# A decoder layer on one core: activations quantised in three passes, through 16-bit integers in the result's place

## The reference, cut to what matters

```python
def _sym_qdq(x, scale):
    s = jnp.clip(jnp.abs(scale), 1e-09, None)
    return jnp.clip(jnp.round(x / s), -(Q_MAX + 1), Q_MAX) * s      # Q_MAX = 7
# _chunk_decompose, on chunks of 64 rows, per chunk and channel
ch_bias = (jnp.max(xp, axis=1, keepdims=True) + jnp.min(xp, axis=1, keepdims=True)) / 2
xz = xp - ch_bias
tmax = jnp.max(jnp.abs(xz), axis=(1, 2)); cmax = jnp.max(jnp.abs(xz), axis=1)
scale = tmax[:, None] / 2.0 ** (DECOMP - 1 - idx) / Q_MAX           # idx from cmax against tmax
result = _sym_qdq(xz, scale[:, None, :])
```

## Time and profile before

| | |
|---|---|
| median of 3 runs | 997.08 us (995.59 to 998.17) |
| the profiled execution | 992.63 us |
| its span, first to last instruction | 990.9 us |
| TensorE, VectorE, ScalarE, GpSimd busy | 757.2, 769.6, 628.0, 116.2 us |
| mean granted clock of TensorE | 0.869 of full speed |

### The profile page before, as it was taken

The page is one execution under the profiler, slowest core; times in us unless marked ns, Lnnn a source line. Parts: engine busy times, 40 slices in busy tenths (PEclk is TensorE's granted clock), DMA queues, the critical chain, the costliest instruction groups (busy, mean ns, idle before and its releaser), DMA issues.

```text
span 990.9 us, 15387 instructions
## 1 busy us (share of the span) xinstructions
PE 757.2 (76%) x5149; PEld 318.5 (32%) x5165; DVE 769.6 (78%) x1055; ACT 628.0 (63%) x1066; POOL 116.2 (12%) x218
## 2 busy tenths in 40 slices
PE   1576988999999999999934824544565559999997
PEld 0432322222222222222311214334334424444443
DVE  7999777999999999999599988688978883632111
ACT  4879435989888888899519217656666746752000
POOL 1200842000000000011000010000002140000001
PEclk9877997999999999999966856567768759999999
DMA  8500864122121212111030001100004830000000
GB/s 297 212 1 1 262 200 129 48 55 56 50 59 49 60 47 58 49 53 33 18 130 0 1 0 43 43 21 22 1 12 176 334 85 1 1 1 2 30 22 32
DMA packets 45733, 66.70 MB, mean 67 GB/s; under 512 B 8940, under 2 KB 23276, under 8 KB 45176
## 3 DMA queue, kind: packets, MB, share of 16 engines
q1 hardware_dynamic: 44408, 61.92, 19.5%
q0 software_dynamic: 1280, 4.20, 1.3%
HBM read 42.50 MB, written 19.14 MB: 62 GB/s over the span
## 4 chain that ended last, share of the span: by engine, by line
PE 50%; DVE 20%; ACT 18%; issue 6%; DMA 3%; POOL 1%; SPq 0%; ACTq 0%; POOLq 0%; DVEq 0%
PE PS L1450 12%; PE PS L1654 8%; PE PS L1665 8%; PE PS L1335 6%; PE PS L1467 6%; ACT slab L1770 4%; ACT slab L1706 2%; PE PS L1364 2%; PE PS L1582 2%; ACT HB L1757 2%; DMA slab<-in_L_ffn_w 2%; DMA slab<-in_x 1%; DVE mx L1039 1%; DVE mx L1038 1%; ACT slab L1677 1%
## 5 line engine op out<-in xcount | busy, mean ns | idle before, releaser
L905 DVE TENSOR_REDUCE SWV<-PS 128x2 f32<-128x1024 f32 x256 | 302.0, 1219 | 16.8 <-PE PS L1335 14.5
L1770 ACT ACTIVATE slab<-PS 128x512 f32<-128x512 f32 x512 | 275.7, 595 | 40.5 <-PE PS L1467 31.5
L1450 PE MATMUL PS<-slab,HB 128*32 128x256 f32 x2048 | 164.3, 393 | 9.9 <-ACT HB L1757 9.6
L1467 PE MATMUL PS<-slab 50*128 50x512 f16 x512 | 125.5, 385 | 3.7 <-ACT slab L1770 1.2
L1335 PE MATMUL PS<-slab 48*128 48x512 f16 x512 | 101.8, 392 | 6.3 <-DVE SWV L905 4.9
L1654 PE MATMUL PS<-slab 128*128 128x512 f16 x384 | 86.2, 388 | 1.7 <-DVE slab L1224 1.4
L1665 PE MATMUL PS<-slab 128*128 128x512 f16 x384 | 83.0, 379 | 0.0
L1450 PEld LDWEIGHTS PS<-slab,HB 128*32 128x32 f32 x2048 | 41.6, 108 | 91.1 <-issue 64.9
L1256 DVE SCALAR_TENSOR_TENSOR WOT<-PS,cmax,WOT 128x512 f32<-128x512 f32 x8 | 6.0, 751 | 69.8 <-PE PS L1665 69.8
L1335 PEld LDWEIGHTS PS<-slab 48*128 48x128 f16 x512 | 24.7, 93 | 104.8 <-issue 95.4
L605 POOL COPY HB<-slab 128x64 f32 (+1 forms) x128 | 24.5, 236 | 285.0 <-PE PS L1450 284.9
(11 more groups left out here) (305 smaller groups left out, 1196.8 us busy)
## 6 DMA issues: line engine op xcount, KB each, us to landing
slab<-in_L_ffn_w SPq DMA_DIRECT2D x2, 4096.0 KB, 14.7
q_split<-slab SPq DMA_DIRECT2D x24, 256.0 KB, 2.7
k_split<-slab SPq DMA_DIRECT2D x24, 256.0 KB, 2.7
slab<-q_split SPq DMA_DIRECT2D x64, 96.0 KB, 2.5
slab<-k_split SPq DMA_DIRECT2D x64, 96.0 KB, 2.5
slab<-in_x SPq DMA_DIRECT2D x4, 1024.0 KB, 12.3
slab<-HB SPq DMA_DIRECT2D x128, 32.0 KB
slab<-in_fside_BxS2xS SPq DMA_DIRECT2D x4, 1024.0 KB, 5.5
```

Source lines behind the costliest of these rows:

```text
L905: nc.vector.tensor_reduce(NM[:, ring].rearrange("p (a x) -> p a x", a=2)[:, :, x], PS[:, bank:bank + 2, :], AX.X, ALU.max, negate=True).th ...
L1450: ins = nc.tensor.matmul(PS[32 * h:32 * h + 32, 6, cols], VST[:, r % 2, k, h, :], PROB[:, k, h, cols], start=k == half == 0, stop=k == KB ...
L1467: nc.tensor.matmul(PS[:, st_bank(2 * s + a), :], KP[rows, r, p, P * k:P * k + P], QP[rows, r, p, :], start=True, stop=True).then_inc(st_re ...
L1770: nc.scalar.activation(PROB[:, k, 2 * a + p], PS[:, st_bank(t), :], ACT.Exp, scale=score_scale).then_inc(probs, 1)
```

## The change

The passes become three on both engines. "scale" and "round" become one: the difference is multiplied by the scale inverse and written as 16-bit integers into the bytes where the bf16 result will stand, the conversion doing the rounding. "back" reads the integers there and writes bf16 over them. On ScalarE the second set of activations has the function Copy with a scale per partition and no bias operand, writes integers, and the single activation at L1710 goes. Since `PASSES` has three entries, VectorE's loops change with it: in the first quantisation `scaled(3)` no longer stands ahead of the last pass but comes after `quantise` and the cast at L900.

```diff
-        PASSES = ("bias", "scale", "round", "back")
+        PASSES = ("bias", "round", "back")
...
-                    if kind == "scale":
-                        own(nc.vector.tensor_tensor(v, v, bc(s["inv"][:, lo:hi]), ALU.mult))
+                    whole = QTF[:, CHUNK * lo:CHUNK * hi]
                     if kind == "round":
-                        own(nc.vector.tensor_scalar(part, part, ROUND, ROUND, ALU.add, ALU.subtract))
+                        own(nc.vector.tensor_tensor(by_chunk(whole.bitcast(I16)), v, bc(s["inv"][:, lo:hi]), ALU.mult))
                     if kind == "back":
-                        nc.vector.tensor_tensor(by_chunk(QTF[:, CHUNK * lo:CHUNK * hi]), v, bc(s["pws"][:, lo:hi]),
+                        nc.vector.tensor_tensor(by_chunk(whole), by_chunk(whole.bitcast(I16)), bc(s["pws"][:, lo:hi]),
                                                 ALU.mult).then_inc(q_dve, 1)
...
-                for bias, scale in ((small["ind"], None), (None, small["inv"])):
-                    if scale:
-                        act.wait_ge(qs_ready, k)
-                    for q in range(lo, hi):
-                        part, _ = quantised(q, q + 1)
-                        nc.scalar.activation(part, part, ACT.Identity, bias=bias[:, q:q + 1] if bias else rnd[:, 0:1],
-                                             scale=scale[:, q:q + 1] if scale else 1.0).then_inc(q_step, 1)
-                    count_q[0] += hi - lo
-                    act.wait_ge(q_step, count_q[0])
-                nc.scalar.activation(a, a, ACT.Identity, bias=rnd[:, 1:2]).then_inc(q_step, 1)
-                count_q[0] += 1
+                for q in range(lo, hi):
+                    part, _ = quantised(q, q + 1)
+                    nc.scalar.activation(part, part, ACT.Identity, bias=small["ind"][:, q:q + 1]).then_inc(q_step, 1)
+                count_q[0] += hi - lo
+                act.wait_ge(q_step, count_q[0])
+                act.wait_ge(qs_ready, k)
+                for q in range(lo, hi):
+                    part, _ = quantised(q, q + 1)
+                    nc.scalar.activation(QTF[:, CHUNK * q:CHUNK * q + CHUNK].bitcast(I16), part, ACT.Copy,
+                                         scale=small["inv"][:, q:q + 1]).then_inc(q_step, 1)
+                count_q[0] += hi - lo
                 act.wait_ge(q_step, count_q[0])
                 for q in range(lo, hi):
-                    part, _ = quantised(q, q + 1)
-                    ins = nc.scalar.activation(QTF[:, CHUNK * q:CHUNK * q + CHUNK], part, ACT.Copy,
-                                               scale=small["pws"][:, q:q + 1])
+                    part = QTF[:, CHUNK * q:CHUNK * q + CHUNK]
+                    ins = nc.scalar.activation(part, part.bitcast(I16), ACT.Copy, scale=small["pws"][:, q:q + 1])
                 ins.then_inc(q_act, 1)
```

More of the change, by code:

```diff
@@ L20 @@
 NI = B * NG
+I16 = mybir.dt.int16
 KB = S // P
@@ L1698, in quantise @@
                 lo, hi = Q_DVE, Q_DVE + Q_ACT
-                a, _ = quantised(lo, hi)
                 act.wait_ge(qb_ready, k)
-                for bias, scale in ((small["ind"], None), (None, small["inv"])):
-                    if scale:
-                        act.wait_ge(qs_ready, k)
-                    for q in range(lo, hi):
-                        part, _ = quantised(q, q + 1)
-                        nc.scalar.activation(part, part, ACT.Identity, bias=bias[:, q:q + 1] if bias else rnd[:, 0:1],
-                                             scale=scale[:, q:q + 1] if scale else 1.0).then_inc(q_step, 1)
-                    count_q[0] += hi - lo
-                    act.wait_ge(q_step, count_q[0])
-                nc.scalar.activation(a, a, ACT.Identity, bias=rnd[:, 1:2]).then_inc(q_step, 1)
-                count_q[0] += 1
+                for q in range(lo, hi):
[9 more added lines that the diff above has]
+                count_q[0] += hi - lo
                 act.wait_ge(q_step, count_q[0])
                 for q in range(lo, hi):
-                    part, _ = quantised(q, q + 1)
-                    ins = nc.scalar.activation(QTF[:, CHUNK * q:CHUNK * q + CHUNK], part, ACT.Copy,
-                                               scale=small["pws"][:, q:q + 1])
+                    part = QTF[:, CHUNK * q:CHUNK * q + CHUNK]
+                    ins = nc.scalar.activation(part, part.bitcast(I16), ACT.Copy, scale=small["pws"][:, q:q + 1])
                 ins.then_inc(q_act, 1)
```

## The result

The changed kernel takes 987.17 us, the median of 6 runs (986.21 to 990.62), against 995.55 (992.33 to 998.17) for the kernel before: a ratio of 0.9915, 95% interval 0.9891 to 0.9939. It is faster, by 8.4 us where 5.3 were forecast, and 987.17 lies under the range. Yet the two profiles differ by 5.6 us only, 985.3 against 990.9 of span, which is nearly the forecast. So there are two questions: where the 5.6 come from, and why the usual gain is larger than that pair shows.

A forecast was written before the change was run, and what follows sets the result against it. Bounds: at k = 1 ScalarE's and VectorE's chains side by side, with GpSimd blocking VectorE's second round; at k = 2 VectorE alone. Savings 2.4 + 2.9 = 5.3 us from the 997.08 median gave 991.8 us, range 988.8 to 995.8.

The forecast's parts named there:

- The price of the integer passes: VectorE's first half, both k: merged integer pass costs no extra over 4.42 us, so 2.29 us are saved.
- rival (c): Slower by 16-bit integers: both new VectorE passes run slow; at half speed 19 us lost, 1016 us; chance 0.05.
- Rival (d): "back" on VectorE runs at double rate, saving a further 2.2 us at each first half, 986.4 us; chance 0.02.
- ScalarE's second set at 8.70, L1710 gone, 5.58 us: ScalarE, both k: 36 activations drop from 12.05 to 8.70 us, L1710 saves 2.23 more, 5.58 in all.
- Turns between VectorE and GpSimd: Second round at k = 1: the engines never run at once; difference 2 precedes the cast, `scaled(3)` starts at 103.6.
- first quantisation: 2.4 us: k = 1: TensorE's step 6 begins about 2.4 us earlier and the rest moves with it; bounds 0.4 and 3.4.
- with TensorE never held, 3.4: Upper bound on the k = 1 saving, 3.4 us, if TensorE's steps are not held up.
- The median as a baseline: The 5.3 us saving, worked out on one profiled execution, was subtracted from the runs' median 997.08, giving 991.8 us.
- The order of worth: k = 1: ScalarE's and VectorE's chains run side by side, neither worth its whole saving alone; VectorE's saving is 2.29 us.
- k = 2, "2.9 us": Second quantisation: TensorE's fifth tile begins 2.9 us earlier as VectorE loses 3.38; bounds 1.2 and 3.4.
- ScalarE at k = 2 gains nothing: ScalarE's saving at k = 2 gains nothing, since TensorE asks for its columns only at tile nine.
- Rival (a), the gains collide: `scaled(3)` waits behind blocked passes and cast, clock rises late at k = 2: about 2.0 us saved, 995.1; chance 0.21.

The follow-up runs named there:

- before_again: The kernel before, unchanged, run and profiled a second time: median 997.03 us, ratio 0.9998.
- second_only: Against the kernel before: three passes on both engines at k = 2 only, four kept at k = 1; 991.89 us, ratio 0.9959.
- before_kp_late: The kernel before, four passes everywhere, with ScalarE's fill of KP moved behind step 2's V eviction; 990.80 us, ratio 0.9956.
- dve_k1: Against the kernel before: three passes on VectorE at k = 1 alone, ScalarE and k = 2 unchanged; 997.87 us, ratio 1.0015.
- act_k2_old: The changed kernel with ScalarE's four passes back at k = 2 alone; 987.09 us, ratio 0.9902 to the kernel before.

## Why the prediction was wrong, point by point

- *The price of the integer passes* (none; rival (c) at 26% more): right. 4.43 and 4.42 us on VectorE. Rival (d), a double rate, did not happen either.
- *ScalarE's second set at 8.70, L1710 gone, 5.58 us*: right. The set took 8.70 us with integer results, and the way back from integers 8.69. From the first of ScalarE's 36 bias activations to the fill of KP it was 31.65 us before (61.90 to 93.55) and 26.04 after (63.10 to 89.14): 5.61.
- *Turns between VectorE and GpSimd*: the mechanism was right, as the rows have it: the cast, asking at 101.62, lost its turn to difference 2, which had asked at 100.25, and ended at 103.76. The trace agrees with the Trainium skill's rule (SBUF — State Buffer, Who interferes with whom) that of two such instructions the one issued first goes first and holds the other up for its whole length. `scaled(3)` came 12.9 us behind `scaled(0)` where I had 13.7, since each turn was 0.1 to 0.2 us shorter than in my sum. The term "first quantisation: 2.4 us" was 3.25 against the same profile. That `scaled(3)` and step 6 began at 103.68 and 108.39, where I had written 103.6 and 108.3, is chance: the passes began 0.96 us later in that profile, which hid the difference. And the bound "with TensorE never held, 3.4" was added up wrongly: from step 2 to step 3 the kernel before took 6.54 us with 1.40 of waiting (93.46 to 100.00), so step 3 could begin at 96.3 and not 96.9, and the bound is 4.0.
- ***The step that failed: the price of the wait at k = 1, in "first quantisation: 2.4 us" with its bounds 0.4 and 3.4.*** I had the row that mattered, `values(2)` waiting for ScalarE, but priced it at its 1.40 us of idle time, with step 2's 3.36 us taken as a fixed length. In the two other profiles of the first quantisation with both engines unchanged (`before_again`, `second_only`), step 2 took 1.90, the wait 3.3, and the clock fell in it, so that `values(2)` and step 3 took 0.85 and 1.55 to 1.6 more. The change removes all of it: 5.8 us, outside my bounds. Removing the wait alone shows it (`before_kp_late`), and so does keeping it (`dve_k1`).
- *The median as a baseline*: "so I subtract from the median" carried a saving worked out against one execution over to the others, whose first quantisation was longer. Besides, the median of the kernel before was 995.55 in the measured comparison, where I had 997.08 from three runs. Of the 4.6 us between 991.8 and 987.17, 1.5 are this, and 3.1 that the change is worth 8.4 and not 5.3.
- *Luck*: my figure for the profiled execution itself, 987.3, was met by 987.03. But this 5.6 is 7.2 in the two stretches less 1.6 elsewhere, so the agreement is in part chance.
- *The order of worth*: I wrote that neither chain is worth its whole saving alone, which holds, but then let VectorE's 2.29 lead the working. Alone it is worth nothing at k = 1 (ratio 1.0015), ScalarE's alone 3.9 us of stretch against `before_again`.
- *k = 2, "2.9 us"*: a mis-sized term, 3.97 measured. VectorE's 3.38 were all had, and 0.6 more. The clock rose during the fourth tile, 1.57 us for its four matmuls in place of 1.89, and no eviction waited, which is about 0.2; the rest is mostly that an eviction with its residual took 1.26 us throughout, where it took 1.28 to 1.29 for the later tiles before, and the cause of that isn't shown. TensorE was at the lower clock for about 10 us from its first tile, not 16. Rows, TensorE's timeline and a window of the changed kernel, against the earlier trace rows:

```profile
541.85 1.57 PE L1512 MATMUL PS<-WB,slab 128*128 128x512 bf16 x4
543.36 0.38 PE L1517 MATMUL PS<-slab,hot 24*128 24x512 bf16 x1
543.73 1.04 PE L1512 MATMUL PS<-WB,slab 128*128 128x512 bf16 x4
```
```profile
543.00:547.00 4.00, 4.00 (x17) 1.20 (x15) 4.00 (x8) 0.00 (x0) 0.00 (x0) 1.00 0.00 0
```

  I had put an early rise of the clock into the bounds (3.4) and chosen the middle. In `before_again` the clock had risen early as well, and TensorE was ahead; it waited 2.06 us for the first eviction, and its next tiles were at the lower clock again (1.89), so that two evictions waited, 0.43 and 0.68 us, and the stretch was 1.0 longer than in the earlier trace rows's profile. It is the course of k = 1 once more:

```profile
552.53 1.89 PE L1512 MATMUL PS<-WB,slab 128*128 128x512 bf16 x4 [2.06 <-DVE HB L970]
```

- *ScalarE at k = 2 gains nothing*: right (`act_k2_old`).
- *Rival (a), the gains collide*: the collisions came, the loss did not.

The sum by the second pair of profiles: 5.76 at k = 1 and 4.99 at k = 2 make 10.75; less 0.8 at the start and a net 0.5 elsewhere, outside the change, gives the 9.5 us between the spans 995.3 and 985.8, which is also the difference of the medians, 996.96 and 987.49.

## What to carry to other kernels

A wait of TensorE is to be priced with what comes after it: here 3.3 us of waiting for one eviction were followed by another 2.4 us lost at the lower clock, and one way to be rid of both was to move 3.6 us of unhurried work behind that eviction. Before a saving is credited to an engine, ask which engine arrives last at the next meeting point; VectorE's 2.3 us were worth nothing until ScalarE's 5.6 were saved. And a forecast in absolute time needs to know where the one profiled execution lies among the runs: this one was near the bottom of a spread of 8 us (992.02 to 1000.27).

## What the runs showed of the hardware

I had not expected that two executions of one kernel could differ by 2.5 us in one stretch with the same instructions, because TensorE's lower clock fell on step 2 (hidden) or on `values(2)` and step 3 (not hidden). Slow matmuls followed TensorE's waits of 3.29, 3.31 and 5.60 us at k = 1 and of 2.06 at k = 2; they didn't follow the waits of 1.40, 1.80 and 2.30 us, and the slow step 2 of the earlier trace rows came behind a wait of 0.92. Why 2.06 had this price and 2.30 had none isn't shown, so the length of a wait alone doesn't tell. A small cast's length depends on its turn: 2.14 us where GpSimd's difference was running, 0.21 in `before_kp_late`, where none was. What moves the time outside the two stretches was not tried. Behind the second one the changed kernel lost 1.7 us against the first profile of the kernel before, but `before_again` lost 1.4 there too, with nothing changed. Up to 36 us behind that stretch these profiles run alike; the loss lies in the next 120 us, the gated product with 8-bit quantisation, where the granted clock of a 30 us window was anywhere from 0.59 to 0.78. So a pair of profiles should be compared stretch by stretch, and not by its spans.
